# FFN prologue of an attention and FFN layer: gate weights loaded in halves, W2 butterflies on VectorE, down projections in front of the next tokens' gates

## The chip, the cores and the metric

The kernel runs on one core of one Trainium2 chip. The time is the device time of one execution in microseconds (us). PE is TensorE, DVE is VectorE, ACT is ScalarE, POOL is GpSimd and SP is SyncE, which here only issues DMAs.

## The reference, cut to what matters

x has 2048 tokens (S) of width 256 (D). The layer adds a causal attention of 16 heads and a gated FFN of 1024 hidden units to x, both computed from the same normalized x.

```python
xn = _layernorm(x, axis=-1)
x = x + _L0_attn_ref(xn, W_K, W_Q, W_V, W_O) + _L0_ffn_ref(xn, W1, W2, W3)

# _L0_ffn_ref
up_gate = jnp.einsum('bsd,hd->bsh', x, W1)
up_lin = jnp.einsum('bsd,hd->bsh', x, W3)
hidden = jax.nn.silu(up_gate) * up_lin
hidden = fwht(hidden)          # Walsh-Hadamard over the 1024 hidden units
out = jnp.einsum('bsh,dh->bsd', hidden, W2)
```

## The kernel before

**Numbers.** Each matmul operand is an fp32 tile split in two: `hi` is the value cast to fp32r, `lo` is the rest. `mm3` multiplies hi by hi, hi by lo and lo by hi (L840 to L842), so each product is three matmuls. A split is always a cast on ACT (`_hi`) and then a subtraction (`_lo`) on DVE or POOL. A `lo` tile of weights lies in `pt_lo`, a `hi` one in `pt_hi`, tiles that the attention needs later.

**Stages.** The program has three stages on PE: the FFN, the projection of all values (`project_values`, 16 tiles of tokens by 4 blocks of 512 columns), and the attention, head after head. No table or planner sets the order. Each engine has its own instruction list, written out by hand in `@block.vector` and so on, and the lists meet only in semaphores.

**The FFN.** Tokens come in four quarters `c` of 512 and the hidden units in eight tiles `t` of 128 (HT = 8). `gate_and_up(c, t)` makes 12 matmuls of 512 columns for the gate (W1) and the up product (W3) into two PSUM banks; two pairs of banks take turns. `silu(c, t)` on ACT (L444) and `multiply(c, t)` on DVE (L679) make `hidden`, `hidden_to_hi` on ACT (L448) and `hidden_to_lo` on DVE (L685, `k_lo<-aux,k_hi`) split it, and `down(c, t)` adds 12 matmuls of 256 columns for W2 into four banks.

**The prologue.** The Hadamard transform is not applied to the hidden units. It is folded into W2 once: four fp32 matmuls with a 128x128 Hadamard matrix (L890), a scaled copy on ACT (L466), three rounds of butterflies, each an addition and a subtraction of 128x1024 on POOL (L344, L345), then the split (L484 on ACT, L351 on POOL). x is normalized from `variances` (L664 to L671, DVE), a square root on ACT (`root`, L434) and `normalize` (L650, DVE, 128x256 each, two to a pair `p` of token tiles). A pair is transposed by PE (`transpose_xn`, L853) and split by `xt_to_hi` (L439) and `xt_to_lo` (L656). Pairs 0 and 1 are the first quarter; pairs 2 to 7 are transposed between the first gate products. Tile `xn` has room for four token tiles, so `normalize(p)` waits until pair `p - 2` has been transposed.

**Places.** W3 is loaded into `w2_b`, the second buffer of the butterflies, so the scaled copy into `w2_b` must wait until W3 has been split. `gate` and `hidden` share `aux` with the raw W1. The values' weights go to `raw` once W2 has been split, and POOL makes both their parts (L410, L413).

## Time and profile before

| | |
|---|---|
| median of 3 runs | 1453.77 us (1450.49 to 1456.17) |
| the profiled execution, its own time | 1447.79 us |
| its span in the trace | 1445.9 us |
| PE busy | 1349.2 us, 93% |
| POOL busy | 970.2 us, 67% |
| DVE busy | 957.3 us, 66% |
| ACT busy | 943.3 us, 65% |

The shares are means over the whole span, which the attention rules with some four fifths of the time. The change touches only what lies before it, so the rows below are almost all from the first 183 us. In a timeline a row is: start, duration, engine, line, operation, output <- inputs, how many, and in brackets how long the engine had been idle and what released it. Matmuls overlap on PE; what a matmul costs is the distance between two starts. A long duration on DVE or POOL can hold a wait for the other engine inside it.

### The profile page before, as it was taken

How to read it: one execution, taken by the hardware profiler on the slowest of the kernel's cores; microseconds unless marked ns; L12 is line 12 of the kernel's file. 1: busy time of each engine (PE TensorE's matmuls, PEld its weight loads, DVE VectorE, ACT ScalarE, POOL GpSimd, SP SyncE). 2: the span in 40 equal slices, each digit the busy share in tenths (PEclk: the TensorE clock that was granted, in tenths of full speed). 3: DMA queues.
4: the chain of work that ended last, by engine and by line, in shares of the span. 5: the costliest groups of instructions: out<-in, count | busy, mean ns of one | idle time of the engine just before them, and what ended most of it. 6: DMA issues, size and time to landing. Idle time of an engine off the chain costs nothing.

```text
span 1445.9 us, 26613 instructions
## 1 busy us (share of the span) xinstructions
PE 1349.2 (93%) x8104; PEld 1187.6 (82%) x8104; DVE 957.3 (66%) x2133; ACT 943.3 (65%) x1911; POOL 970.2 (67%) x628
## 2 busy tenths in 40 slices
PE   3899999979999999999999999999999999999985
PEld 2778888758888888888888888888888888888875
DVE  6743300277777777777777777777777777777760
ACT  3312244457777777777777778787777777777772
POOL 3410000056879787979797978787878797978785
PEclk8999999989999999999999999999999999999998
DMA  4100056579798889897988898889888888888884
GB/s 147 69 1 0 0 146 184 172 222 295 238 293 263 285 270 296 250 290 250 286 267 283 258 288 263 280 258 292 255 281 262 272 281 271 286 270 279 251 265 152
DMA packets 278459, 335.14 MB, mean 232 GB/s; under 512 B 62736, under 2 KB 251280, under 8 KB 273808
## 3 DMA queue, kind: packets, MB, share of 16 engines
q1 hardware_dynamic: 278416, 334.65, 73.7%
q8 instruction: 17, 0.28, 0.1%
q14 instruction: 26, 0.21, 0.0%
HBM read 173.08 MB, written 161.48 MB: 231 GB/s over the span
## 4 chain that ended last, share of the span: by engine, by line
POOL 39%; issue 24%; PE 20%; SPq 6%; DMA 5%; DVE 4%; ACT 2%; POOLq 1%; DVEq 0%; ACTq 0%
POOL pt_lo L375 27%; POOL acc L366 8%; PE ps L840 7%; PE ps L841 6%; PE ps L842 6%; SPq L277 5%; DMA scratch<-raw 3%; POOL v_lo L380 2%; POOL wqk_lo L355 1%; DVE k_lo L685 1%; DMA raw<-w3t 1%; DMA pt_lo<-scratch 1%; ACT raw L551 1%; DVE raw L782 1%; DVE had L772 1%
## 5 line engine op out<-in xcount | busy, mean ns | idle before, releaser
L375 POOL TENSOR_TENSOR pt_lo<-pt_lo,pt_hi 128x640 fp32r<-128x640 f32 (+11 forms) x384 | 661.5, 1752 | 141.2 <-ACT pt_hi L560 141.2
L551 ACT ACTIVATE raw<-ps,had 128x1024 f32<-128x1024 f32 (+7 forms) x384 | 329.1, 866 | 213.4 <-DVE had L775 204.9
L782 DVE STREAM_TRANSPOSE raw<-raw 128x2048 f32<-128x2048 f32 (+15 forms) x256 | 322.0, 1292 | 100.4 <-ACT raw L551 97.9
L840 PE MATMUL ps<-pt_hi,v_hi 128*128 128x256 f32 (+1 forms) x1152 | 326.3, 283 | 20.3 <-POOL pt_lo L375 14.1
L841 PE MATMUL ps<-pt_lo,v_hi 128*128 128x256 f32 (+1 forms) x1152 | 328.4, 285 | 0.0
L842 PE MATMUL ps<-pt_hi,v_lo 128*128 128x256 f32 (+1 forms) x1152 | 326.8, 284 | 0.0
L560 ACT CAST pt_hi<-pt_lo 128x640 fp32r<-128x640 f32 (+11 forms) x384 | 283.2, 818 | 20.7 <-DMA pt_lo<-scratch 20.4
L772 DVE TENSOR_REDUCE had<-ps 128x1 f32<-128x1024 f32 (+1 forms) x256 | 237.9, 949 | 55.4 <-PE ps L842 55.1
L840 PE MATMUL ps<-k_hi,q_hi 128*128 128x512 f32 (+3 forms) x640 | 238.9, 373 | 14.3 <-ACT raw L551 14.3
L840 PEld LDWEIGHTS ps<-pt_hi,v_hi 128*128 128x128 f32 x1152 | 219.5, 191 | 34.6 <-issue 20.8
L842 PE MATMUL ps<-k_hi,q_lo 128*128 128x512 f32 (+3 forms) x640 | 234.3, 366 | 0.0
L841 PE MATMUL ps<-k_lo,q_hi 128*128 128x512 f32 (+3 forms) x640 | 233.8, 365 | 0.0
L841 PEld LDWEIGHTS ps<-pt_lo,v_hi 128*128 128x128 f32 x1152 | 219.1, 190 | 2.2
L842 PEld LDWEIGHTS ps<-pt_hi,v_lo 128*128 128x128 f32 x1152 | 220.5, 191 | 0.0
L380 POOL TENSOR_TENSOR v_lo<-v_next,v_hi 128x512 fp32r<-128x512 f32 x64 | 82.5, 1299 | 170.8 <-ACT v_hi L535 170.8
L366 POOL TENSOR_TENSOR acc<-aux,acc 128x512 f32<-128x512 f32 x128 | 164.8, 1293 | 9.0 <-ACT aux L575 9.0
L840 PEld LDWEIGHTS ps<-k_hi,q_hi 128*128 128x128 f32 x640 | 121.5, 190 | 36.7 <-ACT raw L551 18.8
L842 PEld LDWEIGHTS ps<-k_hi,q_lo 128*128 128x128 f32 x640 | 121.3, 189 | 19.6
L841 PEld LDWEIGHTS ps<-k_lo,q_hi 128*128 128x128 f32 x640 | 121.6, 190 | 18.0
L786 DVE TENSOR_TENSOR z_lo<-ps,z_hi 128x256 fp32r<-128x256 f32 x128 | 54.2, 423 | 123.1 <-ACT z_hi L566 123.1
L767 DVE CUSTOM_DVE_ANT_0 ps<-ps,aux 128x512 f32<-128x512 f32 (+3 forms) x256 | 126.9, 496 | 0.0
L575 ACT ACTIVATE aux<-ps,had 128x256 f32<-128x256 f32 x256 | 108.9, 488 | 3.3 <-PE ps L842 3.3
(102 smaller groups left out, 2205.6 us busy)
## 6 DMA issues: line engine op xcount, KB each, us to landing
all_values<-raw SPq DMA_DIRECT2D x16, 1024.0 KB, 5.0
v_next<-all_values SPq DMA_DIRECT2D x16, 1024.0 KB, 5.5
scratch<-raw SPq DMA_DIRECT2D x64, 256.0 KB, 5.5
pt_lo<-scratch SPq DMA_DIRECT2D x16, 1024.0 KB, 5.2
scratch<-raw SPq DMA_DIRECT2D x64, 240.0 KB, 4.9
pt_lo<-scratch SPq DMA_DIRECT2D x16, 960.0 KB, 5.9
scratch<-raw SPq DMA_DIRECT2D x64, 224.0 KB, 5.2
pt_lo<-scratch SPq DMA_DIRECT2D x16, 896.0 KB, 4.8
```

The costliest lines, as they stand in the source:

```text
L366: pool.tensor_tensor(acc[:, 2 * c:2 * c + 2, :], share[:, z % 2, :, :], acc[:, 2 * c:2 * c + 2, :], ALU.add).then_inc(out_added, 1)
L375: pool.tensor_tensor(lo, lo.bitcast(F32), hi.bitcast(F32), ALU.subtract).then_inc(pt_lo_done, 1)
L380: pool.tensor_tensor(v_lo[:, sl], v_next[:, sl], v_hi[:, sl].bitcast(F32), ALU.subtract).then_inc(v_lo_done, 1)
L551: act.activation(to[:, first // P:(first + n) // P], ps[:, a * BANK:a * BANK + n].rearrange("p (i g k) -> p i g k", g=4, k=BLK), ACT.Exp, ...
L560: act.copy(pt_row(pt_hi, j, a, b), pt_row(pt_lo, j, a, b).bitcast(F32)).then_inc(pt_hi_done, 1)
L575: ins = act.activation(share[:, z % 2, t, :], ring_bank(("O", z))[:, t * D:(t + 1) * D], ACT.Copy, scale=row_rcp[:, j:j + 1])
L767: dve.tensor_tensor_reduce(out=scores, in0=scores, in1=mask[:, BANK - n:], scale=1.0, scalar=-3e38, op0=ALU.add, op1=ALU.max, accum_out=ba ...
L772: dve.tensor_reduce(bank_max[:, j, i:i + 1], scores, AX_X, ALU.max).then_inc(maxed, 1)
L782: dve.transpose(v, v).then_inc(blocked, 1)
L840: pe.matmul(dst, a[0], b[0], start=start, stop=False, skip_group_check=True)
L841: pe.matmul(dst, a[0], b[1], start=False, stop=False, skip_group_check=True)
L842: return pe.matmul(dst, a[1], b[0], start=False, stop=stop, skip_group_check=True)
```

## The change

**Loads.** W1 and W3 are loaded in halves of the hidden units (tiles 0 to 3, tiles 4 to 7). The first halves stand right behind the first quarter of x, the Hadamard matrix and W2 behind the second quarter, and the second halves at the end. W3 has a tile of its own, `w3_raw`; `gate` and `hidden` move to `v_next`, which the attention fills later, and the split hidden units of tiles 4 to 7 to `q_hi` and `q_lo`.

**Engines.** The butterflies and the lo part of W2 move from POOL to DVE, one here and one there between the multiplications of the first quarter. `normalize(p)` for pairs 2 to 7 and three of the four lo halves of the gate weights move from DVE to POOL. The hi part of the values' weights moves to ACT.

**Order.** PE starts with the gates and has the Hadamard matmuls behind tiles 0 and 1. All eight gate tiles of the first quarter now stand ahead of its first down projection. From then on `down(c, t)` stands in front of `gate_and_up(c + 1, t)`. The loops over quarters are written out. `transpose_xn` uses two banks in turn instead of four.

```diff
-        TRANS, RING_AT, Z = 4, 5, 7
+        DOWN, HAD, TRANS = 4, 4, 6
+        RING_AT, Z = 5, 7
...
-        w1_raw, w3_raw = aux[:, :], w2_b
+        w1_raw = aux.rearrange("p (k h) -> p k h", k=KD)
+        w3_raw = sb("w3_raw", [P, KD, HID], F32)
...
-        gate, hidden = ([aux[:, i * BANK:(i + 1) * BANK] for i in pair] for pair in ((0, 1), (2, 3)))
-        hid_hi, hid_lo = k_hi, k_lo
+        gate, hidden = ([v_next[:, i * BANK:(i + 1) * BANK] for i in pair] for pair in ((0, 1), (2, 3)))
...
-        wv_hi, wv_lo = [q_hi, q_lo], [v_hi, v_lo]
+        wv_hi, wv_lo = [pt_hi[:, 3 * S:4 * S], v_hi], [pt_lo[:, 3 * S:4 * S], v_lo]
...
-        PAIRS_AFTER = [(2, 3), (4, 5), (6, 7)] + [()] * (HT - 3)
+        PAIRS_AFTER = {1: (2, 3), 2: (4, 5), 3: (6, 7)}
@@ SP
+            load_x(0)
+            load_gates(0)
+            load_x(1)
+            sp.dma_start(had[:, :], hadamard).then_inc(had_loaded, 16)
+            sp.dma_start(w2_a, w2t.rearrange("p t d -> p (t d)")).then_inc(w2_loaded, 16)
+            load_x(2)
+            load_x(3)
+            load_gates(1)
...
-            sp.wait_ge(w2_lo_done, 1)
+            sp.wait_ge(w2_lo_done, 2)
@@ POOL
-            pool.wait_ge(had_copied, 2)
-            src, dst = w2_b, w2_a
-            for r in range(3):
...
+            def normalize(p):
+                pool.wait_ge(rstd_done, p // 2 + 1)
+                pool.wait_ge(xn_transposed, p - 1)
+                for i in (2 * p, 2 * p + 1):
+                    pool.tensor_scalar(xn[:, i % 4, :], acc[:, i, :], mean_var[:, i, 0:1], rstd[:, i:i + 1],
+                                       ALU.subtract, ALU.mult).then_inc(xn_done, 1)
...
+            gate_weights_to_lo(0, 1)
+            normalize(2)
+            normalize(3)
+            gate_weights_to_lo(1, 0)
+            normalize(4)
+            normalize(5)
+            gate_weights_to_lo(1, 1)
+            normalize(6)
+            normalize(7)
...
-            pool.wait_ge(wv_loaded, 16)
             for k in range(KD):
...
+                for n in range(QUARTERS):
+                    sl = slice(n * BANK, (n + 1) * BANK)
+                    pool.wait_ge(wv_hi_done, 2 * k + n // 2 + 1)
+                    pool.tensor_tensor(wv_lo[k][:, sl], wv_raw[:, k, sl], wv_hi[k][:, sl].bitcast(F32), ALU.subtract
+                                       ).then_inc(wv_lo_done, 1)
@@ ACT
             root(0)
+            gate_weights_to_hi(0, 0)
+            gate_weights_to_hi(0, 1)
             xt_to_hi(0)
             xt_to_hi(1)
...
             root(1)
...
             root(2)
             root(3)
...
             act.activation(table_use[:, 1:2], ones[:, :], ACT.Silu)
...
             for t in range(HT):
                 silu(0, t)
...
                 if t >= 1:
                     hidden_to_hi(0, t - 1)
...
+                if t < 2:
+                    had_copy(t)
+                    gate_weights_to_hi(1, t)
+                for p in PAIRS_AFTER.get(t, ()):
+                    xt_to_hi(p)
+                if t >= 6:
+                    w2_to_hi(t - 6)
...
+                    if c == 1 and t >= 4:
+                        wv_to_hi(t - 4)
@@ DVE
             variances(0)
             normalize(0)
             normalize(1)
+
+            dve.wait_ge(w13_hi_done, 1)
+            dve.tensor_tensor(half(w1_lo, 0), half(w1_raw, 0), half(w1_hi, 0).bitcast(F32), ALU.subtract
+                              ).then_inc(w1_lo_done, 1)
             xt_to_lo(0)
             xt_to_lo(1)
             variances(1)
...
             variances(2)
             variances(3)
...
             for t in range(HT):
                 multiply(0, t)
...
+                for p in PAIRS_AFTER.get(t, ()):
+                    xt_to_lo(p)
+                for n in {1: (0,), 2: (1,), 3: (2,), 4: (3, 4), 5: (5,)}.get(t, ()):
+                    butterfly(n)
+                if t >= 6:
+                    w2_to_lo(t - 6)
...
+                    if t == HT - 1:
+                        add_ffn(c - 1)
@@ PE
             transpose_xn(0)
             transpose_xn(1)
...
             pe.wait_ge(xt_lo_done, 2)
-            pe.wait_ge(w13_lo_done, 2)
-            for t in range(4):
+            pe.wait_ge(w1_lo_done, 1)
+            for t in range(HT):
                 gate_and_up(0, t)
-                for p in PAIRS_AFTER[t]:
+                if t < 2:
+                    had_products(t)
+                for p in PAIRS_AFTER.get(t, ()):
                     transpose_xn(p)
...
+            for c in range(QUARTERS):
                 for t in range(HT):
...
+                    down(c, t)
+                    if c + 1 < QUARTERS:
+                        gate_and_up(c + 1, t)
```

On POOL, before the change, behind the constants at the start of the program stand the butterflies, the lo part of W2 (into `pt_lo`) and the four halves of the values' weights:

```order
L344 TENSOR_TENSOR raw<-raw 128x4x256 [waits had_copied]
L345 TENSOR_TENSOR raw<-raw 128x4x256
L344 TENSOR_TENSOR raw<-raw 128x2x512 [waits w2_summed]
L345 TENSOR_TENSOR raw<-raw 128x2x512
L344 TENSOR_TENSOR raw<-raw 128x1024 [waits w2_summed]
L345 TENSOR_TENSOR raw<-raw 128x1024
L351 TENSOR_TENSOR pt_lo<-raw,pt_hi 128x2048 [waits w2_hi_done]
L410 TENSOR_TENSOR q_hi<-raw,ones 128x2048 [waits wv_loaded]
```

In the changed kernel the same place on POOL has three half-size splits of gate weights and the normalizations (L359 writes `xn`, which is `w_raw`; the row is printed with its first wait):

```order
L366 TENSOR_TENSOR pt_lo<-w_raw,pt_hi 128x2x512 [waits w13_hi_done]
L359 TENSOR_SCALAR w_raw<-acc,raw 128x256 [waits xn_transposed,rstd_done]
L359 TENSOR_SCALAR w_raw<-acc,raw 128x256
L359 TENSOR_SCALAR w_raw<-acc,raw 128x256 [waits xn_transposed,rstd_done]
L359 TENSOR_SCALAR w_raw<-acc,raw 128x256
L366 TENSOR_TENSOR pt_lo<-aux,pt_hi 128x2x512 [waits w13_hi_done]
...
L438 TENSOR_TENSOR pt_lo<-raw,pt_hi 128x512 [waits wv_hi_done] x4
```

The six butterflies have left POOL, and twelve normalizations and three splits of 1024 columns have come to it.

On DVE, in the changed kernel, the stretch from the fourth `variances` (L704 ends it) over the first hidden tiles reads (L712 is `multiply`, L718 `hidden_to_lo`, L689 `xt_to_lo`, L737 a butterfly, L743 the lo part of W2):

```order
L704 RECIPROCAL raw<-raw 128x4 [waits eps_done]
L712 TENSOR_TENSOR v_next<-v_next,ps 128x512 [waits gate_done,up_product] x2
L718 TENSOR_TENSOR k_lo<-v_next,k_hi 128x512 [waits hid_hi_done]
L689 TENSOR_TENSOR xt_lo<-ps,xt_hi 128x2x256 [waits xt_hi_done] x2
L737 TENSOR_TENSOR raw<-raw 128x4x256 [waits had_copied]
...
L737 TENSOR_TENSOR raw<-raw 128x2x512
L737 TENSOR_TENSOR raw<-raw 128x1024 [waits w2_summed]
...
L743 TENSOR_TENSOR pt_lo<-raw,pt_hi 128x1024 [waits w2_hi_done]
```

Before, this stretch of DVE held `normalize` in place of the butterflies and nothing of W2.

On PE, before the change, the list from the second transposition to the first gates and the next transposition reads (L890 is a Hadamard matmul, L840 the first matmul of `mm3`):

```order
L890 MATMUL ps<-raw,had 128x512 [waits w2_loaded,had_loaded]
L890 MATMUL ps<-raw,had 128x512 x3
L840 MATMUL ps<-xt_hi,pt_hi 128x512 [waits hidden_done,w13_lo_done,xt_lo_done]
...
L853 MATMUL ps<-raw,w_raw 128x128 [waits xn_done]
```

In the changed kernel the same stretch is this (L882 is the first matmul of `mm3`, L933 a Hadamard matmul, L893 a transposition):

```order
L882 MATMUL ps<-xt_hi,pt_hi 128x512 [waits w13_lo_done,w1_lo_done,xt_lo_done]
...
L933 MATMUL ps<-raw,had 128x512 [waits w2_loaded,had_loaded]
...
L933 MATMUL ps<-raw,had 128x512 [waits had_copied]
L933 MATMUL ps<-raw,had 128x512
L893 MATMUL ps<-raw,w_raw 128x128 [waits xt_lo_done,xn_done]
L893 MATMUL ps<-raw,w_raw 128x128 x3
```

The Hadamard matmuls now stand behind the gates of tile 0 and tile 1, the second pair of them waits for ACT's copy of the first, and the first transposition of the second quarter stands behind two gate tiles and not one.

## Rows read from the trace of the kernel before

**Rows 1.** Windows: start:end, its length, busy time (instructions) by engine, clock, DMA.
```profile
22.60:80.30 57.70, 42.49 (x216) 35.97 (x217) 46.62 (x58) 15.68 (x27) 36.02 (x11) 0.85 0.12 44
80.30:182.90 102.60, 102.60 (x579) 89.12 (x577) 35.46 (x61) 28.84 (x51) 0.88 (x1) 1.00 0.00 0
182.90:272.50 89.60, 89.60 (x387) 72.08 (x385) 0.73 (x3) 36.92 (x63) 1.24 (x3) 1.00 0.62 176
```

**Rows 2.** Timeline of PE, start of the program.
```profile
9.73 5.10 PE L890 MATMUL ps<-raw,had 128*128 128x512 f32 x8
22.62 0.76 PE L840 MATMUL ps<-xt_hi,pt_hi 128*128 128x512 f32 x1 [7.78 <-DVE had L707]
...
26.17 0.45 PE L842 MATMUL ps<-xt_hi,pt_lo 128*128 128x512 f32 x1
```

**Rows 3.** Timeline of all engines, 13 to 29 us.
```profile
13.45 1.90 ACT L457 CAST pt_hi<-aux 128x2048 fp32r<-128x2048 f32 x1 [3.15 <-DMA aux<-w1t]
...
16.07 1.90 ACT L461 CAST pt_hi<-raw 128x2048 fp32r<-128x2048 f32 x1 [0.61 <-DMA raw<-w3t]
...
18.00 2.29 DVE L704 TENSOR_TENSOR pt_lo<-raw,pt_hi 128x2048 fp32r<-128x2048 f32 x1 [0.33 <-ACT pt_hi L461]
20.33 1.94 ACT L466 ACTIVATE raw<-ps 128x1024 f32<-128x1024 f32 x2 [2.36 <-DVE pt_lo L704]
...
27.21 9.52 DVE L650 TENSOR_SCALAR w_raw<-acc,raw 128x256 f32<-128x256 f32 x4
...
27.55 1.28 ACT L471 ACT_TABLE_LOAD   x1
```

**Rows 4.** Timeline of DVE: the first `variances`, first and last instruction.
```profile
4.35 1.41 DVE L664 BATCH_NORM_STATS2 raw<-acc 128x6 f32<-128x256 f32 x4 [4.35 <-DMA acc<-x]
...
6.41 0.18 DVE L671 RECIPROCAL raw<-raw 128x4 f32<-128x4 f32 x1
```

**Rows 5.** Timelines of DVE and POOL around the values' weights, and PE's wait.
```profile
60.44 3.11 DVE L685 TENSOR_TENSOR k_lo<-aux,k_hi 128x512 fp32r<-128x512 f32 x1
...
69.33 8.21 DVE L685 TENSOR_TENSOR k_lo<-aux,k_hi 128x512 fp32r<-128x512 f32 x2
...
59.40 3.60 POOL L410 TENSOR_TENSOR q_hi<-raw,ones 128x2048 fp32r<-128x2048 f32 x1 [9.01 <-DMA raw<-w_values]
63.08 4.97 POOL L413 TENSOR_TENSOR v_hi<-raw,q_hi 128x2048 fp32r<-128x2048 f32 x1
...
77.60 0.58 PE L840 MATMUL ps<-pt_hi,k_hi 128*128 128x256 f32 x1 [3.25 <-DVE k_lo L685]
```

**Rows 6.** Timeline of PE: gates, one down projection, gates.
```profile
86.20 0.40 PE L840 MATMUL ps<-xt_hi,pt_hi 128*128 x1
...
89.02 0.28 PE L840 MATMUL ps<-pt_hi,k_hi 128*128 128x256 f32 x1
...
90.45 0.39 PE L840 MATMUL ps<-xt_hi,pt_hi 128*128 x1
```

**Rows 7.** Groups by shape on POOL: busy us, mean ns | idle before.
```profile
L360 POOL TENSOR_TENSOR wo_lo<-w_raw,wo_hi 128x256 fp32r<-128x256 f32 x16 | 11.7, 729 | 0.0
L345 POOL TENSOR_TENSOR raw<-raw 128x1024 f32<-128x1024 f32 x3 | 7.1, 2381 | 0.0
...
L417 POOL MEMSET aux<- 128x512 f32 x1 | 0.5, 526 | 0.4 <-DVE acc L693 0.4
L331 POOL TENSOR_SCALAR_AFFINE_SELECT raw<-raw 128x128 f32<-128x128 f32 x1 | 0.3, 293 | 0.2 <-POOL ones L329 0.2
```

**Rows 8.** Groups by shape on DVE and ACT in the first 200 us.
```profile
L679 DVE TENSOR_TENSOR aux<-aux,ps 128x512 f32<-128x512 f32 x32 | 22.0, 687 | 71.2 <-PE ps L842 70.7 <-ACT aux L444 0.2
...
L444 ACT ACTIVATE aux<-ps 128x512 f32<-128x512 f32 x32 | 19.1, 597 | 96.7 <-PE ps L842 96.5
```

**Rows 9.** DMA issues of the first 60 us: size, median us to landing.
```profile
raw<-w_values SPq DMA_DIRECT2D x1, 2048.0 KB, 8.9
```

More of the change, by code:

```diff
@@ L676, in multiply @@
                 dve.wait_ge(gate_done, HT * c + t + 1)
-                dve.wait_ge(hid_lo_done, HT * c + t - 1 + G_FREE)
+                wait(dve, hid_lo_done, HT * c + t - 1)
                 dve.tensor_tensor(hidden[t % 2], gate[t % 2], bank(2 * (t % 2) + 1), ALU.mult
@@ L846, in transpose_xn @@
                 pe.wait_ge(xn_done, 2 * p + 2)
-                if p >= 4:
-                    pe.wait_ge(xt_lo_done, p - 3)
+                wait(pe, xt_lo_done, p - 1)
                 for k in range(KD):
@@ L858, in gate_and_up @@
             def gate_and_up(c, t):
-                pe.wait_ge(hidden_done, HT * c + t - 1 + G_FREE)
+                wait(pe, hidden_done, HT * c + t - 1)
+                if c == 0 and t % 4 == 0:
+                    pe.wait_ge(w13_lo_done, 2 * (t // 4) + 1)
                 for b, hi, lo, done in ((0, w1_hi, w1_lo, gate_product), (1, w3_hi, w3_lo, up_product)):
@@ L880, in down, with had_products @@
                         ins.then_inc(ffn_product, 1)
+            def had_products(i):
+                if i == 0:
+                    pe.wait_ge(had_loaded, 16)
+                    pe.wait_ge(w2_loaded, 16)
+                else:
+                    pe.wait_ge(had_copied, i)
+                for n in range(2):
+                    at = (2 * i + n) * BANK
+                    pe.matmul(bank(HAD + n), had[:, :], w2_a[:, at:at + BANK], start=True, stop=True
+                              ).then_inc(had_product, 1)
             pe.wait_ge(const_ready, 3)
```

175 lines of the change are left out of this document (75 added, 100 removed).

## Prediction

> **What bounds the kernel now.** I read the busy time by engine in windows first, since the change ends where the attention begins. Three stretches tell the story [rows 1]: from the first gate matmul to the end of the first quarter's work PE is busy for 42.5 of 57.7 us at a mean clock of 0.85; in the three quarters behind it for 102.6 of 102.6 us at clock 1.00; in the projection of the values for 89.6 of 89.6 us. So PE bounds everything between 80.3 and 272.5 us, and what can be won lies ahead of 80.3. How much PE work is that? Twelve gate matmuls go from 86.20 to 89.02, 2.82 us, and the twelve of one down projection from 89.02 to 90.45, 1.43 us [rows 6]. A quarter has eight of each, 34.0 us, and the four quarters 136 us. Before, they take from 22.62 to 182.90 [rows 1, 2]: 160.3 us, so 24.3 us are lost inside the FFN, and 22.6 us go by before it. Of the three later quarters 102.6 - 3 x 34.0 = 0.6 us is loop overhead and no more.
>
> Next I read the timelines for what PE waits for. The first gate matmul comes 7.8 us after the last Hadamard matmul [rows 2]. The reader sees the ladder above it [rows 3]: W3 lands at 16.07, ACT casts it in 1.90 us, DVE subtracts in 2.29, ACT copies the Hadamard products in 1.94, and only then may the gates overwrite their banks. PE then runs its first matmuls 0.43 us apart, (26.17 - 22.62) / 8 = 0.44, against 0.235 later [rows 2, 6]: the lower clock level after an idle stretch. Next, DVE's four normalizations take 9.52 us [rows 3]. The arithmetic of one is a small part of it: each sits through a butterfly on POOL of 2.38 us [rows 7]. Last, around the values' weights, `hidden_to_lo` lasts 3.11 and twice 4.1 us, where it starts while POOL works and ends where POOL's instruction does, and PE waits 3.25 us for it [rows 5].
>
> **The change part by part.**
>
> *Start of the gates.* The first 0.5 MB (x) lands at 4.35 [rows 4], 3.1 MB at 13.45 and 4.1 MB at 16.07 [rows 3]. Between these points the new order gives: first halves of W1 and W3 (1.5 MB) about 7.9, second quarter of x 9.7, Hadamard and W2 13.4, third and fourth quarters of x 14.7 and 16.1. ACT casts a half in about 1.05 (1.90 / 2 and a fixed part), from 6.9 to 7.9 and to 9.0. DVE's half of W1, 2.29 / 2 or 1.2, stands behind two normalizations and ends at 9.5. DVE with two SBUF inputs and POOL exclude each other in [rows 5], so POOL's half of W3 comes behind it: 2.38 [rows 7], 9.5 to 11.9. PE starts at 12.0 where it was 22.6. If the halves land a us later, it is 13.0.
>
> *The silu in front.* ACT can't begin it before the roots of all four quarters and the table load, as before. DVE needs 6.59 - 4.35 = 2.24 for one `variances` [rows 4]. The third can start at 14.7, the fourth ends at 19.2; 0.2 for the root and 1.4 for the table [rows 3] give 20.8. PE meanwhile has gates 0 (2.82, and at most 1.75 more for 3.5 us at the lower clock, as at 22.62), two Hadamard matmuls (5.10 us for eight passes at mixed clock, four at the full one 1.72) and gates 1: 12.0 + 4.6 + 1.7 + 2.8 = 21.1. ACT's silu (0.5) and Hadamard copy (1.94 / 2 [rows 3]) end at 22.3, so PE waits 1.2 us. The first-tile clock cost is thus hidden by the silu.
>
> *POOL's chain.* This sets the pace to the fifth tile. ACT goes on with the second half of W1 until 23.4, and POOL subtracts until 25.8. Behind it stand normalizations 4 and 5, the second half of W3, normalizations 6 and 7: eight instructions and one split. No row has this instruction on POOL. The nearest below are one-input ones, 293 ns for 128 columns and 526 for a memset of 512; the nearest above is 729 for 256 columns with two inputs [rows 7]; the groups of 256 and 1024 columns give 2.15 ns a column and 0.18 us fixed, and by 3.60 us for 2048 with one full input [rows 5] it would be 0.43 and 0.18. I take 0.61, with 0.4 and 0.75 as ends: 8 x 0.61 + 2.38 = 7.3 us. In between, DVE has work of the kind that POOL excludes: three `hidden_to_lo` and two butterflies. A butterfly is 1.18 by half of 2.29 [rows 3] and `hidden_to_lo` about 0.6 (0.69 less the overlap [rows 8]): 3 x 0.6 + 2 x 1.18 = 4.2. If both engines take turns, the last normalization ends at 25.8 + 7.3 + 4.2 = 37.3. PE waits for it, 1.7 and 2.7 us before the transpositions, having done gates 2 and 3.
>
> The rows show DVE held by POOL, never clearly POOL held by DVE. The end with POOL never held is worked out by letting the two overlap, and it saves 3.5 us in total, since DVE's chain below then sets the pace. The Trainium skill, SBUF, "Who interferes with whom", says that the one that comes second fully blocks, either way round. By that rule the sum stands as it is; by the one-way reading the time would be 3.5 us shorter. The trace agrees for one direction: 3.11 us where 0.69 is usual.
>
> *To the first down projection.* Transposition, gates 4: 37.3 + 0.5 + 2.8 = 40.6. DVE then has four `multiply` and `hidden_to_lo` pairs less one, three butterflies and the first half of W2's lo part: 7 x 0.6 + 3 x 1.18 + 1.18 = 8.9 less what it did before 40.6; with hand-offs the lo half is ready at 49.2. PE's gates 5 to 7 end at 40.6 + 8.5 = 49.1, so neither waits for the other.
>
> *The rest.* From 49.2 on PE has 32 down projections and 24 gate tiles: 32 x 1.43 + 24 x 2.82 = 113.4 us. Nothing should hold it: ACT and DVE have two instructions of about 0.6 each per 4.25 us of PE [rows 8]. The values' weights are issued at about 51.5, land 8.9 us later [rows 9] and are needed by ACT only at about 67. Their eight POOL splits of 512 columns, 0.18 + 1.10 = 1.3 us, hold DVE by at most 1.3 each, under the slack. The last eight down projections run together, 11.4 us, enough to cover the last tile's ACT and DVE steps. Written-out loops cost nothing by the projection of the values, which is written out and has no gap [rows 1]. The FFN ends at 49.2 + 113.4 = 162.6, less 0.3 for spacings rounded up: 162.3.
>
> **Sum.** The projection starts at 162.3 where it started at 182.9: 20.6 us earlier, 10.6 from the start of the gates and 10.0 from fewer and shorter waits. Everything behind it is unchanged. The profiled execution took 1447.8 us, so it would be 1427.2. The median of the runs, 1453.8, is 6.0 above that execution, a spread of the attention's. The forecast is the median less 20.6: **1433 us**.
>
> **Bounds.** Normalizations at 0.4 or 0.75 us: 1.8 less or 1.1 more. Port one-way: 3.5 less. The quarters of x later by 2 us, since pieces of 2 KB may move slower than whole rows: 1.8 more. A fall of the clock at the wait of 2.7 us (it fell before at one of 3.25 [rows 5]): 1.7 more. The spread of three runs is 5.7 us. Together the leading case has 1427 to 1439.
>
> **The rivals.**
> 1. *POOL longer on the path* (0.22). Normalizations of 1.3 us, the two-input price of 512 columns and more than any row speaks for, cost about 10 x 0.7 = 7 us (eight on POOL's chain, and of pairs 2 and 3 what then holds their transpositions), and 1.7 us 11: 1440 to 1444. For it: two scalar operands read per row, on an engine that no row shows doing so. Against: every row of POOL goes by columns with a small fixed part. The Trainium skill, GPSIMD Engine Reference, "Engine selection", is against elementwise work on GpSimd, about 2x slower with two inputs and near line rate with one; the trace has 2381 against half of 2.29 us for the subtraction. By that page the moved normalizations would be nearer my lower end.
> 2. *More than forecast* (0.06). POOL never held and all halves landing early: PE-bound from 12.0, with the one wait of 1.2, it would be at 158 at the end: 25 us, 1428 or less.
> 3. *Hardly any change* (0.07). A new stall takes the place: ACT waits for the values' weights inside the second quarter with silus queued behind it, or the slower normalizations meet the late x. It would need over 13 us of new waits, 1447 to 1461. Against: the slack of some 7 us at the weights.
> 4. *Slower* (0.03). The twelve normalizations are so slow on POOL that each pair holds a transposition. With ten on the chain the gain is gone at 0.61 + 20.6 / 10 = 2.7 us each, and the kernel is 0.5% slower from 3.4 us; at 4 us the time is 1433 + 34 = 1467. Against: 729 ns for the dearest row of that width [rows 7].
>
> **How the numbers follow.** The leading case has 0.62. Range 1426 to 1443 takes in rival 1's nearer part and most of rival 2. A measurement of this kernel can tell about 0.5%, 7.3 us, from no change. Faster by more: 0.62 + 0.22 + 0.06 = 0.90; within: 0.07; slower: 0.03.
>
> **What would show it.** First gate matmul at 12 to 13; silu at about 21; POOL's normalizations at 0.6 each with longer ones beside a butterfly; the first down projection at 47 to 52; no idle PE from there to the projection of the values at about 162, at clock 1.00. The forecast is wrong if a normalization on POOL lasts over 1 us, if silus wait in the second quarter, or if PE's distances between matmuls are not 0.235 and 0.119 there.

## The result, and the profile of the changed kernel

The changed kernel's median is 1432.3 us (1430.08 to 1434.14, 4 runs) and that of the kernel before, on the same chip, 1452.13 us (1447.55 to 1456.17, 4 runs). The ratio is 0.9858, 95% interval 0.9834 to 0.9882. The changed kernel is faster by 1.2 to 1.7%. The profiled execution took 1434.14 us, its span is 1432.3.

Windows of the changed kernel come first. They answer to [rows 1], cut at its own stages.

```profile
12.00:50.00 38.00, 30.13 (x116) 22.17 (x117) 24.26 (x51) 16.18 (x29) 21.43 (x14) 0.96 0.18 58
50.00:165.00 115.00, 114.94 (x675) 101.14 (x675) 42.15 (x68) 36.22 (x60) 13.60 (x9) 1.00 0.05 19
165.00:255.00 90.00, 90.00 (x394) 72.66 (x393) 1.50 (x4) 36.65 (x63) 0.82 (x2) 1.00 0.61 173
```

PE is again busy from the first down projection (53.10) to the end of the FFN, and what it loses lies ahead of 53 us. (The clock's readings in this trace begin at 15.8 us; a window ahead of that prints 1.00 without a reading.) Its timeline shows where; these are the rows that begin a wait or a stage, and they answer to [rows 2] and, by its last row, to the third window of [rows 1].

```profile
11.98 0.76 PE L882 MATMUL ps<-xt_hi,pt_hi 128*128 128x512 f32 x1 [2.30 <-POOL pt_lo L366]
...
21.96 1.98 PE L933 MATMUL ps<-raw,had 128*128 128x512 f32 x4 [0.70 <-ACT raw L483]
...
28.20 0.66 PE L893 MATMUL ps<-raw,w_raw 128*128 128x128 f32 x4 [0.57 <-POOL w_raw L359]
...
31.23 0.66 PE L893 MATMUL ps<-raw,w_raw 128*128 128x128 f32 x4 [2.37 <-POOL w_raw L359]
...
37.17 0.66 PE L893 MATMUL ps<-raw,w_raw 128*128 128x128 f32 x4 [2.47 <-POOL w_raw L359]
...
39.57 1.07 PE L893 MATMUL ps<-raw,w_raw 128*128 128x128 f32 x4 [1.75 <-POOL w_raw L359]
40.29 0.78 PE L882 MATMUL ps<-xt_hi,pt_hi 128*128 128x512 f32 x1
40.87 0.63 PE L883 MATMUL ps<-xt_lo,pt_hi 128*128 128x512 f32 x1
...
43.00 0.44 PE L882 MATMUL ps<-xt_hi,pt_hi 128*128 128x512 f32 x1
...
53.10 0.36 PE L882 MATMUL ps<-pt_hi,k_hi 128*128 128x256 f32 x1
...
166.28 0.39 PE L882 MATMUL ps<-pt_hi,xt_hi 128*128 128x512 f32 x1
```

The reader sees three things. The gates start 10.6 us earlier than in [rows 2]. The four transpositions of pairs wait for POOL's normalizations (L359), 7.2 us together. And after two waits close to each other the matmuls from 40.3 to 43.0 are 0.43 us apart, as behind the long wait in [rows 2]: the granted clock there is 0.50, the 1.2 GHz level. The window says so:

```profile
40.30:42.90 2.60, 2.60 (x8) 2.12 (x7) 1.60 (x2) 0.59 (x1) 0.00 (x0) 0.50 0.39 106
```

The matmuls of the first gate tile, up to 15.5 us, stand just as far apart.

POOL's timeline shows what the transpositions wait for. These rows stand where [rows 3] has the butterflies' time; L359 is a normalization, L366 the split of half a gate weight.

```profile
13.69 4.83 POOL L359 TENSOR_SCALAR w_raw<-acc,raw 128x256 f32<-128x256 f32 x4 [1.85 <-ACT raw L459]
22.92 2.38 POOL L366 TENSOR_TENSOR pt_lo<-aux,pt_hi 128x1024 fp32r<-128x1024 f32 x1 [4.40 <-ACT pt_hi L479]
25.27 5.90 POOL L359 TENSOR_SCALAR w_raw<-acc,raw 128x256 f32<-128x256 f32 x4
31.14 2.40 POOL L366 TENSOR_TENSOR pt_lo<-w_raw,pt_hi 128x1024 fp32r<-128x1024 f32 x1
33.53 5.99 POOL L359 TENSOR_SCALAR w_raw<-acc,raw 128x256 f32<-128x256 f32 x4
```

The group of all twelve, by its line, gives least, median and greatest duration in ns:

```profile
L359 POOL TENSOR_SCALAR w_raw<-acc,raw x12: 1213/1220/2188, 13.7 to 38.3; 128x256 f32<-128x256 f32 x12
```

The first four, while DVE runs `variances` from one input, take 1.21 us each. The other eight take 1.49 on the mean, and POOL has no gap from 22.92 to 39.52. DVE's timeline shows what of that is contention (L718 is `hidden_to_lo`, L737 a butterfly).

```profile
24.04 1.81 DVE L718 TENSOR_TENSOR k_lo<-v_next,k_hi 128x512 fp32r<-128x512 f32 x1
...
27.67 1.22 DVE L737 TENSOR_TENSOR raw<-raw 128x1024 f32<-128x1024 f32 x1
28.80 0.68 DVE L712 TENSOR_TENSOR v_next<-v_next,ps 128x512 f32<-128x512 f32 x1
29.40 0.68 DVE L718 TENSOR_TENSOR k_lo<-v_next,k_hi 128x512 fp32r<-128x512 f32 x1
```

Beside POOL's subtraction (22.92 to 25.30) `hidden_to_lo` lasts 1.81 where 0.68 is usual. Beside POOL's normalizations the butterfly lasts 1.22 and `hidden_to_lo` 0.68: DVE is not held by them. POOL is: of the eight, the four that meet a butterfly or a `hidden_to_lo` last 1.68, 1.84, 2.19 and 1.41, the other four 1.21 to 1.22.

**The marker used below.** Executions of one kernel differ by up to 12 us, and the stretch from the first matmul of the values' projection to the end of the span took between 1260.1 and 1268.5 us in the twelve profiles of whole kernels here, in no order that goes with the edits. So the experiments are read first by when the values' projection starts, in PE's timeline: 182.90 us before, 166.28 in the changed kernel.

### The profile page after: what moved, and what is told of

It reads as the page before. It is cut to its first block, busy times and chain, and to the rows that moved or that the text cites. A ratio compares the mean times of both kernels' runs of the same rounds, so it can differ in the third digit from the quotient of the medians.

```text
span 1432.3 us, 26483 instructions
## 1 busy us (share of the span) xinstructions
PE 1351.3 (94%) x8104; PEld 1192.5 (83%) x8104; DVE 937.6 (65%) x2125; ACT 947.6 (66%) x1918; POOL 969.9 (68%) x640
## 4 chain that ended last, share of the span: by engine, by line
POOL 38%; issue 23%; PE 22%; SPq 7%; DMA 5%; DVE 2%; ACT 2%; POOLq 1%; ACTq 0%; DVEq 0%
POOL pt_lo L401 26%; POOL acc L392 8%; PE ps L882 7%; PE ps L883 7%; PE ps L884 7%; SPq L297 6%; DMA scratch<-raw 4%; POOL v_lo L406 2%; ACT raw L587 1%; POOL wqk_lo L381 1%; DVE raw L824 1%; DMA pt_lo<-scratch 1%; POOL w_raw L359 1%; DVE had L814 1%; DMA acc<-x 1%
## 5 line engine op out<-in xcount | busy, mean ns | idle before, releaser
L882 PE MATMUL ps<-pt_hi,v_hi 128*128 128x256 f32 (+1 forms) x1152 | 328.4, 285 | 19.4 <-POOL pt_lo L401 13.2
L882 PE MATMUL ps<-k_hi,q_hi 128*128 128x512 f32 (+3 forms) x640 | 239.5, 374 | 13.1 <-ACT raw L587 13.1
L882 PEld LDWEIGHTS ps<-pt_hi,v_hi 128*128 128x128 f32 x1152 | 222.3, 193 | 32.4 <-issue 18.7
L884 PEld LDWEIGHTS ps<-pt_hi,v_lo 128*128 128x128 f32 x1152 | 223.6, 194 | 0.0
L882 PEld LDWEIGHTS ps<-k_hi,q_hi 128*128 128x128 f32 x640 | 122.0, 191 | 35.1 <-ACT raw L587 17.2
```

The costliest lines, as they stand in the source:

```text
L882: pe.matmul(dst, a[0], b[0], start=start, stop=False, skip_group_check=True)
L884: return pe.matmul(dst, a[1], b[0], start=False, stop=stop, skip_group_check=True)
```

## The experiments

All but three start from the changed kernel: w3_place starts from the kernel before, and pool_alone and pool_alone2 are programs of their own. The runs were made in four groups, each on one chip and with runs of the kernel before beside them. The medians of before are 1452.13 us beside the changed kernel, 1451.95 beside the runs from again to spread, 1452.84 (one run) beside twice, bf_pool and load_old, and 1449.54 beside the last three rows. So medians of different groups are not compared closely. Times of PE in us from the span's start:

| kernel | gates | first down | values' projection | median (range, runs) | ratio to before, 95% |
|---|---|---|---|---|---|
| before | 22.62 | 51.11 | 182.90 | 1452.13 (1447.55-1456.17, 4) | |
| changed | 11.98 | 53.10 | 166.28 | 1432.3 (1430.08-1434.14, 4) | 0.9858, 0.9834-0.9882 |
| again | 12.06 | 52.24 | 165.43 | 1431.38 (1428.55-1436.34, 6) | 0.9866, 0.9841-0.9891 |
| norm_early | 13.08 | 46.55 | 159.73 | 1429.91 (1427.81-1431.0, 5) | 0.9847, 0.9824-0.9871 |
| norm_dve | 11.97 | 47.82 | 160.99 | 1428.45 (1423.54-1434.63, 4) | 0.9854, 0.9823-0.9885 |
| spread | 13.74 | 48.98 | 162.17 | 1430.71 (1430.37-1432.47, 4) | 0.9854, 0.9827-0.9881 |
| twice | 12.87 | 66.22 | 179.39 | 1441.29 (one run) | |
| bf_pool | 13.53 | 56.59 | 169.77 | 1434.17 (one run) | |
| load_old | 17.29 | 57.00 | 170.19 | 1437.91 (one run) | |
| order_old | 12.62 | 53.74 | 167.90 | 1434.08 (1429.6-1436.75, 4) | 0.9885, 0.9849-0.9922 |
| w3_place | 22.18 | 48.60 | 180.25 | 1449.09 (1442.51-1454.14, 10) | 0.9992, 0.997-1.0014 |
| early_spread | 12.13 | 45.62 | 158.79 | 1425.58 (1424.98-1428.4, 6) | 0.9831, 0.9805-0.9856 |

The difference of two columns tells most: from the first down projection to the values' projection it is 113.17 to 113.19 us in every kernel with the changed order. Whatever those edits do, they do ahead of the first down projection. Before and w3_place have only four of the eight gate tiles ahead of it, so their times in that column can't be set beside the others.

**again.** The changed kernel once more, beside the others.

> The changed kernel once more, timed in five rounds, as the reference of the variants that follow. In its first trace the projection of the values starts at 166.28 us where before it started at 182.90, 16.6 us earlier. If that is the whole effect, the median difference to the kernel before is 16 to 18 us. If something behind the FFN changed as well, it is 20 us or more, and the stretch from the start of the projection to the end is shorter than the 1263.0 us of before.

It starts the projection at 165.43, 0.85 us earlier than the first profile and 17.5 before the kernel before. Its median is 20.6 us below that of before on its chip, which was expected only if the stretch behind had become shorter, and that took 1262.4 us for 1263.0. So again some 3 us of the medians' difference show in no profile. Differences of the marker below a us or two say nothing unless their cause is in a row. One such cause is the landing of W1's first half. ACT casts it from 6.73 us in the changed kernel's first profile and only from 8.71 in spread, with the same loads in the same order; the gates start 11.98 and 13.74.

**norm_early.** The normalizations of pairs 2 to 7 on DVE, ahead of the first hidden tile. They don't have to wait for late transpositions, since pairs 2 to 5 have places of their own (the raw gate weights, once these are split; not in the cut).

```diff
@@ POOL
-            normalize(2)
-            normalize(3)
...
@@ DVE
+            normalize(2)
+            normalize(3)
             variances(2)
             variances(3)
+            for p in range(4, 8):
+                normalize(p)
             for t in range(HT):
                 multiply(0, t)
```

> Normalizations of pairs 2 to 7 back on VectorE, right behind the variances, into free halves of the raw gate weights. Theory A (GpSimd's normalizations at 1.22 us, not 0.61, hold the transpositions): the waits of 0.6, 2.4, 2.5 and 1.7 us before the transpositions and the fall of the clock go, the first down projection starts at 46 to 47 and the values' projection at 159 to 160. Rival B (VectorE's own list sets the pace, and the normalizations only show it): 4 us more of VectorE work, no gain, 166 to 168.

Start of the projection: 159.73, 5.7 to 6.6 us earlier than in the changed kernel although its gates start a us later. No transposition of pairs 2 to 7 waits any more, and the granted clock is 1.00 from 20 to 60 us, where the changed kernel has 3.4 us at 0.50. The normalizations on POOL are what the FFN's first quarter waits for.

**norm_dve.** The same move with the places as they are: DVE normalizes a pair when the pair two before it has been transposed, as in the kernel before, and POOL keeps only its splits of weights.

```diff
@@ DVE
             variances(3)
+            normalize(2)
+            normalize(3)
...
                 for p in PAIRS_AFTER.get(t, ()):
                     xt_to_lo(p)
+                    if p + 2 < TILES // 2:
+                        normalize(p + 2)
```

> Normalizations back on VectorE at their places of the kernel before, between the splits of the transposed pairs, all else as changed. Theory A: 12 times 0.37 us on VectorE in place of 12 times 1.22 on GpSimd; values' projection at 161 to 163. Rival B: VectorE's list is 4.4 us longer, 168 to 171.

160.99, at the lower edge of the expected range. So it is not DVE's time that is short; the engine that normalizes decides. On DVE one takes 0.41 us, by the group of the four of pairs 0 and 1 in the changed kernel:

```profile
L683 DVE TENSOR_SCALAR w_raw<-acc,raw 128x256 f32<-128x256 f32 x4 | 1.4, 408 | 0.3 <-ACT raw L459 0.3
```

**spread.** Normalizations stay on POOL; the transpositions of pairs 4 to 7 stand behind one gate tile each.

```diff
-        PAIRS_AFTER = {1: (2, 3), 2: (4, 5), 3: (6, 7)}
+        PAIRS_AFTER = {1: (2, 3), 2: (4,), 3: (5,), 4: (6,), 5: (7,)}
```

> Pairs 4 to 7 are transposed singly behind gate tiles 2 to 5 and not two by two behind tiles 2 and 3; the normalizations stay on GpSimd. Theory A: the chain on GpSimd is as long, but the gates of tile 4 wait only for the weights and not for normalizations 6 and 7; values' projection at 164 to 165, 1.5 to 2.3 us earlier than 166.3. Rival B: no change, 166 to 167.

162.17, earlier than expected, with gates that start 1.8 us late. POOL's list is as long as in the changed kernel, but PE has a gate tile to do while it waits. The waits for `w_raw` shrink from 7.2 to 0.8 us, and one of 2.07 before tile 4 comes, for POOL's last split of a weight. None of them lowers the clock, which is 1.00 from 20 to 60 us, so part of the gain is the clock's.

**twice.** Each normalization on POOL is made twice, with the same values.

```diff
+                    pool.tensor_scalar(xn[:, i % 4, :], acc[:, i, :], mean_var[:, i, 0:1], rstd[:, i:i + 1],
+                                       ALU.subtract, ALU.mult).then_inc(xn_once, 1)
+                    pool.wait_ge(xn_once, i - 3)
                     pool.tensor_scalar(xn[:, i % 4, :], acc[:, i, :], mean_var[:, i, 0:1], rstd[:, i:i + 1],
                                        ALU.subtract, ALU.mult).then_inc(xn_done, 1)
```

> Each of the 12 normalizations on GpSimd is done twice, with the same result. Theory A (they stand on the path, some ten of them): 10 to 12 us more, the values' projection at 176 to 180. Rival B (VectorE sets the pace): within 2 us of 166.3.

PE's waits in the trace of this kernel, sum, number and longest, by who releases it:

```profile
PE ps L897 <- POOL w_raw L363: 16.1, 4, 5.3
```

179.39 is 13.1 to 14.0 us later than in the changed kernel, within the expected range, and 0.8 to 0.9 of it is the start of the gates. The waits grow by 8.9 to 10.1 us, from 7.2 and 6.0. The rest goes with the clock: it is at 0.50 from 32.9 to 43.1 and from 46.5 to 56.7 us, 20 us in place of 3.4. That PE pays 12 to 13 us for twelve instructions of 1.22, 14.6 in all, is thus the sum of two effects, and not the price of each instruction passed on.

**bf_pool.** The butterflies on POOL again, between and behind the normalizations.

```diff
@@ POOL
             gate_weights_to_lo(1, 1)
+            butterfly(0)
             normalize(6)
             normalize(7)
+            for n in range(1, 6):
+                butterfly(n)
@@ DVE
-                for n in {1: (0,), 2: (1,), 3: (2,), 4: (3, 4), 5: (5,)}.get(t, ()):
-                    butterfly(n)
```

> The six butterflies back on GpSimd, behind its last split of gate weights, with normalizations 6 and 7 behind the first of them. All else as changed. If moving the butterflies is what brings the gain of the first quarter, the transposition of pair 6 waits 2.4 us more and W2 comes later: values' projection at 169 to 175. If VectorE is relieved by as much as GpSimd is burdened, it stays at 166.

169.77 lies in the expected range, but 1.5 us of the 3.5 to 4.3 are a late landing of W1 (gates at 13.53). From the gates to the first down projection it is 43.06 us where the changed kernel has 41.12 and again 40.18. The move of the butterflies is thus worth 2 to 3 us here, by one profile and at this place in POOL's list.

**load_old.** The loads in the old order: Hadamard matrix and W2 ahead of the first halves of the gate weights.

```diff
             load_x(0)
-            load_gates(0)
-            load_x(1)
             sp.dma_start(had[:, :], hadamard).then_inc(had_loaded, 16)
             sp.dma_start(w2_a, w2t.rearrange("p t d -> p (t d)")).then_inc(w2_loaded, 16)
+            load_x(1)
+            load_gates(0)
             load_x(2)
```

> Loads in the order of before: Hadamard, W2 and the second quarter of x ahead of the first halves of the gate weights. Everything else as changed. The first half of W3 lands at about 13.4 and the gates start at 16.5 to 17.5 in place of 12.0. If the start of the gates is worth its full distance (the prediction counted 10.6 us for it), the values' projection starts 4.5 to 5 us later, at 171. If the silu behind the roots hides it, it starts 1 to 2 us later, at 167 to 168.

The gates start 5.3 us later, at 17.29, and the projection 3.9 to 4.8 us later (against the two profiles of the changed kernel), at 170.19. So 0.5 to 1.4 of the 5.3 us are hidden, and the expectation that the first silu hides most of it fell. The traces show why: that silu (L469) itself moves from 20.41 to 25.07. DVE's list has the split of W1's first half (L751) ahead of the other `variances`. It waits there for ACT's cast, and the roots, the table load and the silu come later by nearly as much. From load_old's timelines:

```profile
13.38 1.23 DVE L751 TENSOR_TENSOR pt_lo<-aux,pt_hi 128x1024 fp32r<-128x1024 f32 x1 [5.10 <-ACT pt_hi L479]
...
25.07 0.58 ACT L469 ACTIVATE v_next<-ps 128x512 f32<-128x512 f32 x1
```

**order_old.** In the later quarters gates ahead of down projections again, and the sums at the quarter's end.

```diff
-            for c in range(QUARTERS):
+            for t in range(HT):
+                down(0, t)
+            for c in range(1, QUARTERS):
                 for t in range(HT):
-                    down(c, t)
-                    if c + 1 < QUARTERS:
-                        gate_and_up(c + 1, t)
+                    gate_and_up(c, t)
+                    if t >= 2:
+                        down(c, t - 2)
+                down(c, HT - 2)
+                down(c, HT - 1)
```

> The changed kernel with the order of the later quarters put back: the first quarter's eight down projections run together, then each quarter has its gates ahead of its downs, and the sums into the residual stand at the quarter's end. If that order brings nothing because PE has no wait there either way (theory), the values' projection starts at 165.3 to 167.5 us (165.4 and 166.3 in the two profiles of the changed kernel) and the median stays within 1430 to 1435. If the order carries part of the gain (rival), it starts at 170 or later, with waits of PE for a DVE sum or hidden part between the quarters.

(The cut shows PE's part; on DVE the four sums go back behind their quarter.) 167.90, a little beyond the theory's range and well short of the rival's; 0.6 of it is the start of the gates. From the first down projection on it takes 114.16 us instead of 113.18. The order of the later quarters is worth 1.0 us. That all eight gate tiles of the first quarter stand ahead of its down projections was left in place here, and no run tries it by itself.

**w3_place.** From the kernel before, W3 in a tile of its own alone.

```diff
-        w1_raw, w3_raw = aux[:, :], w2_b
+        w1_raw, w3_raw = aux[:, :], sb("w3_raw", [P, KD * HID], F32)[:, :]
@@ ACT
             root(1)
-            act.wait_ge(w3_loaded, 16)
-            act.copy(w3_hi, w3_raw).then_inc(w13_hi_done, 1)
-
-            act.wait_ge(w13_lo_done, 2)
             for i in range(2):
...
+            act.wait_ge(w3_loaded, 16)
+            act.copy(w3_hi, w3_raw).then_inc(w13_hi_done, 1)
             root(2)
```

> The kernel before with one part of the change: W3 in a tile of its own, so that ACT's scaled Hadamard copies stand ahead of the cast of W3 and wait for no split. The butterflies then start some 4 to 5 us earlier. If the butterflies on POOL are what stretches DVE's normalizations (9.5 us for four), these get free of them sooner and the values' projection starts at 176 to 180 instead of 182.9. If the place alone brings nothing, because the gates still wait for both splits (rival), it starts at 182 to 184, or later where the cast of W3 comes 2 us later and holds the first gates: 184 to 186.

180.25: 2.65 us, between the theory's and the rival's ranges. POOL's first butterfly starts at 17.34 instead of 22.35 us. Of DVE's timeline of w3_place two rows answer to the one of 9.52 us in [rows 3]:

```profile
26.84 7.40 DVE L648 TENSOR_SCALAR w_raw<-acc,raw 128x256 f32<-128x256 f32 x4
...
35.36 0.72 DVE L648 TENSOR_SCALAR w_raw<-acc,raw 128x256 f32<-128x256 f32 x2
```

Four normalizations still take 7.40 us, since butterflies still run beside them, until 33.77; the two at 35.36, behind the last butterfly, take 0.72 together. In the times nothing can be told from no change, ratio 0.9992, as 2.65 of 1450 us would have it.

**early_spread.** The edits of norm_early and spread together.

> Two edits together: the normalizations early on DVE in places of their own, and pairs 4 to 7 transposed one behind each gate tile. Alone they let the values' projection start at 159.7 and 162.2 where the changed kernel has 165.4 and 166.3. If their gains add up as far as PE's own work allows (theory), it starts at 156.5 to 159: gates at 13.1 plus 136 us of products, 2.5 of transpositions and Hadamard passes, the first silu's wait and the lower clock. If the early normalizations already took all there was (rival), it starts at 159.5 to 161. The whole then is 1424 to 1428, if the stretch behind takes 1266 us as in the mean of the profiles so far.

158.79, in the range of the theory, and the median is in its range too. PE's waits from the first gates to 55 us, in its timeline:

```profile
12.13 0.76 PE L890 MATMUL ps<-xt_hi,pt_hi 128*128 128x512 f32 x1 [2.52 <-POOL pt_lo L372]
22.62 1.98 PE L941 MATMUL ps<-raw,had 128*128 128x512 f32 x4 [0.82 <-ACT raw L483]
45.62 0.36 PE L890 MATMUL ps<-pt_hi,k_hi 128*128 128x256 f32 x1 [1.58 <-issue]
```

No transposition of pairs 2 to 7 waits. This version beats the kernel before clearly. Against the changed kernel the marker is 6.6 to 7.5 us earlier and the median 5.8 to 6.7 us lower, but in another group on another chip, where before was 2.4 us faster too, and the intervals of the two ratios to before overlap. The nearest comparison on one chip is with order_old, the changed kernel but for 1.0 us: its fastest of four runs, 1429.60, is above the slowest of six here, 1428.40.

**pool_alone.** Nothing of the layer is computed: POOL runs normalizations and other instructions by themselves, then 16 normalizations beside eight products of 1024 columns on DVE, both inputs in SBUF.

```python
for n in (128, 256, 512, 1024):
    for i in range(3):
        pool.tensor_scalar(ts_two[:, at:at + n], src[:, at % 2048:at % 2048 + n], other[:, 0:1],
                           other[:, 1:2], ALU.subtract, ALU.mult)
```

> A kernel of its own, without the layer's computation: on GpSimd tensor_scalar with two column operands for 128, 256, 512 and 1024 columns, with one operand, with constants, and tensor_tensor for 256 and 1024; then 16 tensor_scalar of 256 columns beside 8 tensor_tensor of 1024 columns with two SBUF inputs on VectorE. Theory A1 (a fixed start-up makes up the 1.22 us): about 1.0 fixed, 1024 columns at 1.5 to 1.8 us, and constants in place of column operands cheaper. Theory A2 (a price by column): 128 columns at 0.7, 1024 at 4.3 us, 4 ns a column. Beside VectorE: if each instruction excludes the other, the two lists add up, 16 x 1.22 + 8 x 1.15 = 28.7 us; if not, 19.5 us.

The groups by shape of this kernel (L50 a normalization, L55 with one column operand, L58 with two constants, L61 and L64 a product of two tiles, L67 the normalizations beside DVE's L78):

```profile
L67 POOL TENSOR_SCALAR both_pool<-src,other 128x256 f32<-128x256 f32 x16 | 25.6, 1608 | 0.0
L50 POOL TENSOR_SCALAR ts_two<-src,other 128x1024 f32<-128x1024 f32 x3 | 11.3, 3782 | 0.0
L78 DVE TENSOR_TENSOR both_dve<-src,other 128x1024 f32<-128x1024 f32 x8 | 9.9, 1307 | 45.0 <-POOL tt_out L64 45.0
...
L64 POOL TENSOR_TENSOR tt_out<-src,other 128x1024 f32<-128x1024 f32 x2 | 4.6, 2340 | 0.0
L50 POOL TENSOR_SCALAR ts_two<-src,other 128x256 f32<-128x256 f32 x3 | 3.6, 1222 | 0.0
...
L58 POOL TENSOR_SCALAR ts_imm<-src 128x256 f32<-128x256 f32 x3 | 3.2, 1074 | 0.0
L55 POOL TENSOR_SCALAR ts_one<-src,other 128x256 f32<-128x256 f32 x3 | 2.7, 925 | 0.0
...
L61 POOL TENSOR_TENSOR tt_out<-src,other 128x256 f32<-128x256 f32 x3 | 2.1, 724 | 0.0
```

Alone a normalization takes 1222 ns, as in the kernel: that is its price, not contention. It goes by columns, as in theory A2: (3782 - 1222) / 768 = 3.33 ns each and 0.37 us fixed, where a product of two tiles has (2340 - 724) / 768 = 2.10 and 0.19. Beside DVE's products the sixteen normalizations take 25.6 us, between the 19.5 without exclusion and the 28.7 with the full one. The first three, which lie beside most of DVE's 9.9 us, last 2.27, 3.75 and 3.62 us.

**pool_alone2.** Two more pairings, again without the layer's work (the cut shortens the slices).

```python
# on POOL, 16 times each                          # on DVE, 8 and 16 times
pool.tensor_tensor(out_a, src, other, ALU.mult)   # dve.tensor_tensor(dve_a, src, other, ALU.mult)
pool.tensor_scalar(out_b, src, ...)               # dve.tensor_tensor(dve_b, src, ps, ALU.mult)
```

> Only the two engines, none of the layer's work: 16 subtractions-like products of two tiles, 256 columns, on POOL beside 8 of 1024 columns on DVE; then 16 normalizations of 256 columns on POOL beside 16 products of 512 columns on DVE with one input in PSUM. Alone a POOL product takes 0.72 us, a normalization 1.22, a DVE product of 1024 columns 1.14 to 1.2. If either engine's instruction excludes the other's whole (the both-way reading), the first pair needs 16 x 0.72 + 8 x 1.18 = 21 us for both; if they only slow each other where they meet, 12 to 16. In the second pair DVE has one SBUF input: if that is free of POOL, POOL's mean stays at 1.22; if any DVE product with a tile in SBUF holds POOL, it is 1.5 or more, as it was beside products of two tiles (1.61).

```profile
L57 POOL TENSOR_SCALAR out_b<-src,other 128x256 f32<-128x256 f32 x16 | 19.3, 1222 | 0.0
L50 POOL TENSOR_TENSOR out_a<-src,other 128x256 f32<-128x256 f32 x16 | 18.8, 1210 | 0.0
L71 DVE TENSOR_TENSOR dve_a<-src,other 128x1024 f32<-128x1024 f32 x8 | 13.3, 1736 | 7.3 <-POOL mark L47 7.3
L77 DVE TENSOR_TENSOR dve_b<-src,ps 128x512 f32<-128x512 f32 x16 | 9.7, 681 | 5.5 <-POOL mark L54 5.5
```

With one input in PSUM (L77) neither engine notices the other: 1222 and 681 ns, their usual durations. In product beside product (L50, L71) both are slowed, and the pair is done after 18.8 us, between the expectation without exclusion, 12 to 16, and the full one, 21.

## Why the prediction was right, and where it was off

**The median** came out at 1432.3 for a forecast of 1433, but part of that is luck. In the traces the FFN gives 182.90 - 166.28 = 16.6 us where 20.6 were forecast. The medians differ by 19.8. The other 3.2 us show in no profile: the stretch behind took 1263.0 us before and 1266.0 after, against the sign of the medians' difference, and the profiled execution of before was 4.3 us faster than its own median. In the second group of runs they are 3.1 us again (20.6 for 17.5 by again's marker), in the fourth there is nothing of the kind (order_old: 15.5 for 15.0). What makes executions differ there stayed open. The base moved as well, from 1453.8 (three runs) to 1452.1 (four).

**Where the 16.6 us lie.** 10.6 are the start of the gates, as forecast; inside the FFN it is 6.0 for a forecast of 10.0. By PE's rows the waits there fall from 15.3 us (8.4 for normalizations, 4.8 for `hidden_to_lo` beside the values' weights, 2.1 ahead of the first down projection) to 7.9, and the four Hadamard matmuls, which before lay ahead of the gates, add 3.1. The clock helps: before, it is at 0.50 up to 26.3, from 29.7 to 39.9 and for 3.4 us from 77.5. The experiments price the loads (3.9 to 4.8), the butterflies (2 to 3), W3's place in the kernel before (2.65) and the later quarters' order (1.0). The move of the values' weights to ACT and their split into pieces were not tried alone; only the rows speak for them: the two waits of together 4.8 us are gone.

**Start of the gates, 12.0.** Right: 11.98, and in the order foretold: ACT's two casts from 6.73 and 8.36, DVE's half, then POOL's half from 9.49 for 2.35 us. "If the halves land a us later, it is 13.0" was needed too: 11.97 to 13.74 in nine profiles with the new loads. load_old shows what of it the new order of loads gives: 5.3 us of the 10.6.

**The first silu.** Forecast 20.8, it starts at 20.41; PE's wait for the Hadamard copy was 0.7 instead of 1.2. That this silu hides the first tile's slow matmuls fits both profiles: PE waits for the copy behind it until 21.96 in the one, and reaches it at 22.30 in the other (again), just as the copy ends at 22.25. It doesn't hide late gate weights, since it moves with them (load_old). The bound for later quarters of x wasn't needed: the third quarter's `variances` start at 14.06, for 14.7.

**POOL's chain: the term that was mis-sized.** It is "8 x 0.61 + 2.38 = 7.3 us". A normalization takes 1.22 us, outside the bounds of 0.4 and 0.75 and beyond the "over 1 us" by which the prediction called itself wrong; the term measures 8 x 1.22 + 2.40 = 12.2. PE's waits for it are 7.2 us where 1.7 and 2.7 were forecast. (The bound for 0.4 us is 8 x 0.21 = 1.7 and not 1.8.) The prediction took its duration from rows of other instructions of the same width, and the nearest of them, 729 ns [rows 7], was too low as an upper end. Rival 1 had nearly the right price, 1.3 us, and too high a bill, 7 us.

**The hold of 4.2 us** in the same chain was too large, and that is why rival 1's bill didn't come. From 25.27 to 39.52 POOL needs 14.25 us; 12.2 are its own, so 2.1 are waits for DVE. They sit on four normalizations: the one of 1675 ns lies beside the `hidden_to_lo` of 24.04, that of 1836 beside the butterfly of 27.67 and the next `hidden_to_lo`, that of 2188 beside the butterfly of 33.15, and that of 1408 beside the `hidden_to_lo` of 35.34. DVE's instructions with one input in PSUM, `multiply` and `xt_to_lo`, cost POOL nothing, as pool_alone2 shows. With 4.9 us more for the term, 2.1 less for the hold and a start 0.5 earlier, the last normalization ended at 39.5, and not 37.3: 2.2 us of the 4.0 that the forecast missed. Two errors of opposite sign cancelled in part, which is luck too.

**The clock.** The bound "a fall of the clock at the wait of 2.7 us: 1.7 more" came true, at waits of 2.47 and 1.75. From the end of the last normalization to the first down projection it is 13.6 us instead of 11.9, and the six steps from 40.29 to 43.00 take 2.71 us where six of 0.235 are 1.41, which explains 1.3 of these 1.7. In again, with 6.0 us of waits instead of 7.2, the marker is 0.85 us earlier, and the clock falls elsewhere: it is at 0.50 from 31.7 to 35.1, behind the waits of 0.58 and 2.37, and stays at 1.00 behind those of 0.80 and 2.23.

**Ports, both ways or one way.** The Trainium skill, SBUF, "Who interferes with whom", says that a DVE instruction with two SBUF inputs contends with a GpSimd instruction that reads SBUF, and one with at most one SBUF input, outside its two-port modes, doesn't. The runs agree with the second half (POOL 1222 and DVE 681 ns) and with the first for two products (1210 for 724, 1736 for about 1220). That whoever comes second fully blocks the section says of the two-port modes. With the full exclusion that the prediction drew from it for two SBUF inputs the case of this change doesn't agree: beside DVE's products POOL's normalizations lose 25.6 - 19.3 = 6.3 us, and the eight products take 9.9 us, 1.24 each, the duration of one undisturbed (1.22, L737). So POOL is held by DVE and DVE is not held by a normalization, though POOL's was first by 0.1 us. The prediction had said that the rows show POOL held by DVE "never clearly", and both readings that it weighed, turns in full and no hold at all, were too simple.

**Engine selection.** The Trainium skill, GPSIMD Engine Reference, "Engine selection", gives about 2x for two inputs, and there the trace agrees: 2340 against 1220 ns for 1024 columns. Of one input it says near line rate. That doesn't hold for this instruction: 1222 ns on POOL against 408 on DVE, three times, and its price is above that of a product of two tiles (724).

**The rest, 113.1 us without a wait.** Right to 0.1: 113.18, and 113.17 to 113.19 in nine profiles. The values' weights landed 7.8 us after their issue at 55.5 and ACT took them at 74.1, with no silu behind them late. The written-out order of later quarters brought little, as the prediction had it (0.6 us of overhead to win): 1.0 us.

**The rivals.** More than forecast (158 for the start of the projection) is nearly reached by early_spread, 158.79, once the normalizations are off the path. Hardly any change and slower needed 13 us of waits or 2.7 us per normalization; twice, at 2.44 us for each, brings the marker to 179.39, 3.5 us ahead of before, which fits the stated turning point. Its one timed run, 1441.29, is 11.5 us ahead of before all the same, since the stretch behind the marker took 1260.1 us, the shortest of all.

## What to carry to other kernels

Before a step is moved to another engine, its price there has to come from that instruction with its kinds of operands; the nearest row of the same width with other operands, 729 ns, was off by a factor of 1.7, and the estimate by two. An engine that is free by its busy share can still be the one that PE waits for, when its instruction takes three times as long and stands in a chain between two PE steps. In such a chain look for independent PE work to put in front of the wait: one line that spreads the transpositions gave 3 to 4 us, more than half of the 4.4 to 6.6 that moving the work back gave. A step that seems to hide a delay hides nothing when it hangs on the same load: follow its inputs first, as load_old shows.

## What the runs showed of the hardware beyond that

- A normalization with two column operands on POOL costs 0.37 us and 3.33 ns a column; with one column operand 925 ns for 256 columns, with two constants 1074, a product of two tiles 724.
- POOL's normalizations lose 6.3 us beside 9.9 us of DVE products with both inputs in SBUF, up to 3.75 us for one of 1.22, and hardly slow them. POOL's products slow DVE's from 1.24 to 1.67 us each (13.35 / 8) and are slowed themselves from 0.72 to 1.21. What in the instruction makes that difference was not tried.
- The same load, second in the queue, let ACT begin at 6.73 to 8.71 us in executions of kernels whose loads are the same. That alone moves the start of the gates by 1.8 us.
